# A recommendation kernel on one core: a longer TensorE loop, front rows earlier, 75 columns, and VectorE's first pick ahead of its high one-hot

## What is computed

```python
user_emb = table_user[user[:, 0]]
item_emb = concat([table_i1[item[:, 0]], table_i2[item[:, 1]], table_i3[item[:, 2]]])
ub = concat([table_i1[his[:, :, 0]], table_i2[his[:, :, 1]], table_i3[his[:, :, 2]]])
q = broadcast(item_emb)
h = concat([q, ub, q - ub, q * ub]) @ w_att1.T + b_att1
score = where(his[:, :, 0] == 0, 0.0, h @ w_att2.T + b_att2)
browse = einsum('bl,ble->be', score, ub)
x = dice(concat([item_emb, browse, user_emb]) @ w1.T + b1, a1, g1, be1)
x = dice(x @ w2.T + b2, a2, g2, be2)
out = sigmoid(x @ w3.T + b3)
```

## Time and profile before

| | |
|---|---|
| median of three runs | 1789.54 us |
| profiled execution | 1791.8 us |
| its span (first to last instruction) | 1790.0 us |
| TensorE busy | 1531.2 us, 86% |
| VectorE busy | 1462.4 us, 82% |
| GpSimd busy | 1272.0 us, 71% |
| ScalarE busy | 1177.5 us, 66% |
| mean granted TensorE clock | 0.946 of full speed |

### The profile page before, as it was taken

One profiled execution on the slowest core, in us unless ns is written; L12 is line 12 of the kernel. 1 busy time (PEld: TensorE's weight loads), 2 busy tenths in 40 slices (PEclk: granted clock), 3 DMA queues, 4 the chain that ended last, 5 costly groups with the idle time before them and its releaser, 6 DMA issues. The chain is left out here.

```text
span 1790.0 us, 76739 instructions
## 1 busy us (share of the span) xinstructions
PE 1531.2 (86%) x31007; PEld 1410.1 (79%) x31007; DVE 1462.4 (82%) x1514; ACT 1177.5 (66%) x1921; POOL 1272.0 (71%) x1988
## 2 busy tenths in 40 slices
PE   5798989899897988989799798988979798898975
PEld 4788878788787888878788787888878788887862
DVE  6699887979787797888879788797888789889964
ACT  5576766667575676766567576676756567675546
POOL 3588677877776786777777777787777677767850
PEclk8799999999898999999899899999999899899986
DMA  2111020211102011120201102011110201102000
GB/s 35 50 50 52 25 75 19 72 28 43 49 25 67 23 50 43 28 73 16 76 23 47 46 25 67 26 49 41 46 56 16 77 22 50 43 24 73 22 21 0
DMA packets 33047, 74.85 MB, mean 42 GB/s; under 512 B 15471, under 2 KB 20463, under 8 KB 28911
## 3 DMA queue, kind: packets, MB, share of 16 engines
q1 hardware_dynamic: 25656, 68.48, 13.2%
q0 software_dynamic: 2144, 1.36, 0.8%
q10 hardware_dynamic: 4952, 0.28, 0.2%
HBM read 7.02 MB, written 0.01 MB: 4 GB/s over the span
## 5 line engine op out<-in xcount | busy, mean ns | idle before, releaser
L755 ACT ACTIVATE hiT<-hiT_ps 128x800 bf16<-128x800 bf16 x512 | 429.6, 839 | 352.2 <-PE hiT_ps L514 346.4
L550 PE MATMUL wsum_ps<-scaled_lo,onehot_hi 100*128 100x78 bf16 x12288 | 553.0, 201 | 60.3 <-DVE scaled_lo L986 56.7
L974 DVE TENSOR_REDUCE score_j<-sel 100x24 f32<-100x600 f32 x512 | 397.4, 776 | 253.0 <-PE sel L536 251.3
L536 PE MATMUL sel<-scoretab,hiT 128*128 128x75 bf16 x12288 | 540.3, 202 | 69.7 <-DMA scoretab<-scores_b 63.6
L536 PEld LDWEIGHTS sel<-scoretab,hiT 128*128 128x128 bf16 x12288 | 501.6, 100 | 122.9 <-issue 86.2
L550 PEld LDWEIGHTS wsum_ps<-scaled_lo,onehot_hi 100*128 100x128 bf16 x12288 | 509.2, 100 | 75.7 <-DVE scaled_lo L986 65.8
L986 DVE TENSOR_TENSOR scaled_lo<-onehot_lo,parts 100x3744 bf16<-100x3744 bf16 x256 | 546.3, 2134 | 19.3 <-POOL parts L424 15.0
L763 ACT ACTIVATE wsum_ring<-wsum_ps 128x300 f32<-128x300 f32 x512 | 359.9, 703 | 185.2 <-PE wsum_ps L550 151.1
L410 POOL TENSOR_TENSOR score<-score_j 100x16 f32<-100x16 f32 x256 | 236.4, 923 | 329.0 <-DVE score_j L974 325.7
L514 PE MATMUL hiT_ps<-identb,onehot_hi 100*128 100x100 bf16 x4096 | 274.0, 211 | 88.5 <-issue 76.2
L413 POOL TENSOR_TENSOR score<-score,score_j 100x16 f32<-100x16 f32 x256 | 318.5, 1244 | 20.1
(11 more groups left out here) (158 smaller groups left out, 1017.6 us busy)
## 6 DMA issues: line engine op xcount, KB each, us to landing
scoretab<-scores_b SPq DMA_DIRECT2D x96, 375.0 KB
weightsum<-wsum_ring SPq DMA_DIRECT2D x128, 125.0 KB
weightsum<-wsum_ring SPq DMA_DIRECT2D x64, 150.0 KB
raw<-in_r_rec_his_dram SPq DMA_DIRECT2D x32, 150.0 KB, 2.6
item_rows<-in_L_rec_table_i_dram,ids_now POOLq DMA_INDIRECT x51
table_blk<-in_L_rec_table_i_dram SPq DMA_DIRECT2D x3, 125.0 KB
user_rows<-in_L_rec_table_user_dram,ids_now POOLq DMA_INDIRECT x16, 4.1
weightsum<-in_L_rec_w_dram ACTq DMA_DIRECT2D x6, 25.0 KB
```

Source lines behind the costliest of these rows:

```text
L536: mm = pe.matmul(o, rows, scoretab[0:HJ, s // 16, :, b, i, :], start=(i == 0), stop=(i == 2))
L550: mm = pe.matmul(wsum_ps[:, b * U:(b + 1) * U], hi_columns(n % 4, g), scaled_lo[:, n % 2, g, i % 3, :], start=(i == 0), stop=(i == 5))
L755: act.activation(hiT[:, s % 2, 0:8 * POS], hiT_ps[:, 0:8 * POS], ACT.Copy).then_inc(hiT_copied, 1)
L974: dve.tensor_reduce(score_j[:, n % 2, g0:g0 + 8, :].rearrange("p (q c) j -> p q (c j)", q=2), sel[0:POS, 2 * (s % 2):2 * (s % 2) + 2, 0:4 ...
```

## The change

Four edits, each in one engine's program.

1. TensorE's loop has seven tiles in its body and runs twice, in place of one tile and fourteen times. The other engines' loops stay at one tile.
2. ScalarE's front rows of even slots come right behind the copy of `hiT`, ahead of the task, the sums and the split copy.
3. The sum matmuls read 75 of the 78 columns of the product (three runs of 25) and write them without gaps; ScalarE's copy reads them without gaps.
4. VectorE's pick of slot 2n comes before the high one-hot of step n + 1.

```diff
+        RUN = 7
...
-                        mm = pe.matmul(wsum_ps[:, b * U:(b + 1) * U], hi_columns(n % 4, g),
-                                       scaled_lo[:, n % 2, g, i % 3, :], start=(i == 0), stop=(i == 5))
+                        mm = pe.matmul(wsum_ps[:, b * W:(b + 1) * W].rearrange("p (j v) -> p j v", j=NF), hi_columns(n % 4, g),
+                                       scaled_lo[:, n % 2, g, i % 3, :].rearrange("p (j v) -> p j v", j=NF)[:, :, 0:LO],
+                                       start=(i == 0), stop=(i == 5))
...
-            with pe.Fori(1, TILES - 1) as t:
-                for s in range(SLOTS):
-                    slot(t, s)
+            with pe.Fori(0, (TILES - 2) // RUN) as run:
+                for i in range(RUN):
+                    for s in range(SLOTS):
+                        slot(run * RUN + (i + 1), s)
...
-                               .rearrange("p (j l) b -> p b j l", j=NF),
-                               wsum_ps[:, 0:4 * U].rearrange("p (b j l) -> p b j l", b=4, j=NF)[:, :, :, 0:LO], ACT.Copy
+                               .rearrange("p u b -> p b u"),
+                               wsum_ps[:, 0:4 * W].rearrange("p (b u) -> p b u", b=4), ACT.Copy
...
                     copy_hiT(t, s + 1)
                 elif not last:
                     copy_hiT(t + 1, 0)
+                if s % 2 == 0 and s < SLOTS - 2:
+                    lo_rows(t, s // 2 + 1)
+                elif s % 2 == 0 and not last:
+                    lo_rows(t + 1, 0)
...
                     split_copy(i // 3, i % 3, 3 * NR * (t + 1) + i + 1)
-                if s % 2 == 0 and s < SLOTS - 2:
-                    lo_rows(t, s // 2 + 1)
-                elif s % 2 == 0 and not last:
-                    lo_rows(t + 1, 0)
...
             def step(t, n, last=False):
+                pick(t, 2 * n)
                 if n < STEPS - 1:
                     onehot_high(t, n + 1)
                 elif not last:
                     onehot_high(t + 1, 0)
-                pick(t, 2 * n)
                 onehot_low(t, n)
                 pick(t, 2 * n + 1)
```

More of the change, by code:

```diff
@@ L246, in build @@
         EARLY = 3
+        RUN = 7
+        assert (TILES - 2) % RUN == 0
         ctx.enter_context(nc.allow_non_contiguous_dma(reason="a few hundred weights and ids, loaded once"))
```

## The result

The changed kernel takes 1670.12 us (median of four runs, 1669.42 to 1674.73) against 1790.78 for the kernel before in the same comparison: a ratio of 0.933, with a 95% interval of 0.930 to 0.936. The forecast was 1671. The sum came out within 1 us, but none of its four terms did, as the experiments show: two were too small, one too large, and one had been put at nothing.

What follows compares the result with a forecast made beforehand. No engine is full: TensorE and VectorE lead in turn, with a floor of about 5.3 us a step. Jumps 59, front rows 53, columns 8 and pick 0 sum to 120 us: 1790.0 to 1670, forecast 1671, range 1642 to 1712.

Steps and rivals of the forecast that it cites:

- the 0.7 us on top of the stall: TensorE's jumps back: each costs 0.7 us beyond its 4.25 stall, 4.95 in all; 12 removed jumps give 59 us.
- No fetch: Rival: idle pieces at tile boundaries do not come from the jump and stay; 1730 us, chance 0.05.
- The 76.2 us are of this kind: TensorE's idle time before transposes is waiting for ScalarE's front rows, about 5.1 us in each of 15 tiles.
- My share of 70%: Part of the transposes' idle time that moving the front rows gains at the end: 53 us of 76.2.
- 0.04 us a slot: Sum matmuls of 75 columns take 0.85 us against 0.89 for 78; over 210 slots, 8 us gained.
- GpSimd's chain starts from the second pick, which does not move. I take 0.: VectorE's pick before the high one-hot: GpSimd's chain is unaffected, so the edit gains or costs 0 us.
- the 0.10 us of room before the product: In the last tile GpSimd's last piece ends 0.10 us before VectorE's product starts; both are at about 5.3 us a step.
- part 2: ScalarE's front rows moved ahead of the sums: 3.5 us in each of 15 tiles, 53 us gained.
- Pace: Rival: VectorE and GpSimd take back what the front rows free; 60 us gained, 1731, halfway 1700; chance 0.16.
- the clock (0.961): Sign of being right: TensorE's granted clock above 0.97.
- VectorE's wait (105.3 for 130): Sign of being right: VectorE's wait for the scores near 130 us, from 251.3 before.
- the 0.85 us of the sum group: Sign of being right: 24 sum matmuls on TensorE take 0.85 us, against 0.89 before.

Runs made afterwards that it cites:

- the old order: Changed kernel with VectorE's high one-hot again ahead of the pick of slot 2n: 1652.17 us, ratio 0.923 to the kernel before.

## Why the prediction was right, and where it was not

The total was right by terms that cancel, and that it came within 1 us is luck. (By its own sum it would have been 1669.5: 1789.5 less 120.)

| term | forecast | alone on before | undone on the changed kernel |
|---|---|---|---|
| loop of seven tiles | -59 | -67 | not run |
| front rows | -53 | -77 | -67 |
| 75 columns | -8 | -2 (same) | -2 (same) |
| pick first | 0 | +18 | +18 |
| sum, or the whole | -120 | -128 | whole: -121 |

- **Jumps.** Right in mechanism: the idle pieces belong to the jumps, and the straight boundaries have none. The size of one was low, 4.95 against 5.6. The step that was mis-sized is the 0.7 us on top of the stall. It was read from one jump (tile 6 to 7), and that is one of the two cheapest of the 13: from product to product it costs 3.2 us, with a stall of 3.06, where the others go up to 7.7. On the mean of all 13 jumps 1.2 us come on top of the stall of 4.25. "No fetch" is refuted.
- **Front rows.** Right in mechanism, too small. The failed step is "The 76.2 us are of this kind": with the 0.16 us hidden in each modelled end it is 105, and 77 us less the 7.6 behind the jumps are two thirds of that. My share of 70% was about right, the quantity was not. The steps show where: over tiles 1 to 14, steps 3 to 6, with the finish and layer 1, give 2.3 us a tile (I had put 2), and steps 1, 2, 7 and 8 give 1.6 (I had put 1.5). I had taken every other step for one of 5.61 that can only fall to 5.3. But step 10, which has the digit tasks, lasts 6.83 and falls to 5.74, 15 us in all, and the boundary (steps 14 and 15) gives 5 us.
- **Columns.** The step "0.04 us a slot" failed: the difference of the two groups in the earlier trace rows was taken for the price of three columns. The rule of the Trainium skill (Advanced Engine Details and Errata, PSUM Cachelines) was not borne out as a significant loss: at most some 0.03 us a group can be charged to the gaps.
- **Pick first.** This is the one step whose mechanism was wrong: "GpSimd's chain starts from the second pick, which does not move. I take 0." The chain's start does not move, but its operations run in the gaps between VectorE's, and those did move; it cost 18 us both alone and on top of the rest. I had read the 0.10 us of room before the product in the earlier trace rows and used it only against part 2.
- **Pace.** That rival's mechanism appeared (50.1 us of the product waiting for GpSimd), but not from the freed pace alone: in the old order it is 13.0 us with the front rows and the loop in place. The fourth edit alone makes it 30.3, and with the pace freed as well 50.1. In TensorE's wait for the product the freed pace shows directly, 90.1 us with the front rows alone against 56.7.
- **The whole.** The terms alone make 128, the whole 121. The seven in between fit the overlap of the first two edits at the boundaries, the 7.6 us above.
- **Signs.** One jump's piece left, the transposes' idle time under 20 us, tiles of 96 to 99 us (but for the one with the jump and the last two) and more waits for GpSimd came true; the clock (0.961), VectorE's wait (105.3 for 130) and the 0.85 us of the sum group did not.

## What to carry to other kernels

A total that fits does not show that its terms do: run each edit alone, or undo each, even when the time comes out as forecast. Here one of four edits cost 18 us and one did nothing, and leaving the bad one out, writing out TensorE's last loop and moving one small mask gave 38 us more. Where a chain on one engine runs in the gaps of another, the order of that other engine's operations is part of the chain, though no semaphore says so. Read lateness from start to start of like groups, not from the idle column, where ends are modelled.

## What the hardware did that I had not expected

- GpSimd operations of 0.22 us last 0.69 to 1.97 us beside VectorE's bf16 operations between SBUF tiles, and 0.22 to 0.25 beside a pick from PSUM. The mean of one operation in the chain (L422) is 431 ns in the old order and 730 in the changed kernel, with nothing but two of VectorE's operations exchanged.
- A jump back over a TensorE body of some 3,900 instructions costs 5.6 us in all (the one over a body seven times as long 4.6), while VectorE's loop of fewer than 200 rows showed none: the product of 779.51 ends at 781.6, and its next one-hot starts at 781.54, across VectorE's own jump.
- Matmuls of 78 columns in one run and 75 in three both take 37 ns from start to start, those of 50 in two runs 25 ns.
